# One product of 256 columns for the scores, and another order of a step's work in attention

## The reference, cut

```python
q = rmsnorm(q, q_norm_w); k = rmsnorm(k, k_norm_w)
q = apply_rope(q, rope_cos, rope_sin); k = apply_rope(k, rope_cos, rope_sin)
scores = einsum('bhtd,bhsd->bhts', q, k) * scale
scores = LOGIT_SOFTCAP * tanh(scores / LOGIT_SOFTCAP)
scores = where(mask, -inf, scores)
attn = softmax(scores, axis=-1)
out = einsum('bhts,bhsd->bhtd', attn, v)
return out @ wo.T
```

## Time and profile before

| | us |
|---|---|
| median of 3 runs | 2193.07 |
| lowest and highest | 2185.72, 2206.43 |
| the profiled execution, its own time | 2193.82 |
| its span in the trace | 2192.1 |
| PE busy, and PE weight loads | 2042.5 (93%), 1828.2 (83%) |
| DVE, ACT, POOL busy | 1085.6 (50%), 949.4 (43%), 1039.2 (47%) |
| granted TensorE clock, mean | 0.975 |

### The profile page before, as it was taken

One profiled execution on the slowest core, in us unless ns is written; L12 is line 12 of the kernel. 1 busy time (PEld: TensorE's weight loads), 2 busy tenths in 40 slices (PEclk: granted clock), 3 DMA queues, 4 the chain that ended last, 5 costly groups with the idle time before them and its releaser, 6 DMA issues.

```text
span 2192.1 us, 41896 instructions
## 1 busy us (share of the span) xinstructions
PE 2042.5 (93%) x12188; PEld 1828.2 (83%) x12189; DVE 1085.6 (50%) x2355; ACT 949.4 (43%) x2127; POOL 1039.2 (47%) x1070
## 2 busy tenths in 40 slices
PE   3999999999999999999968997899999999999997
PEld 2888888888888888888857886889999999988886
DVE  5555545555667676767545546333333333332322
ACT  4555545554565565656534410233333333333322
POOL 3444434442444445454546206367643223588864
PEclk9999999999999999999878998999999999999999
DMA  8877767777777776756324226467544333489898
GB/s 311 291 247 250 245 227 242 257 240 278 270 260 260 291 266 238 275 205 231 113 84 166 87 86 218 153 215 252 198 139 143 119 118 120 153 201 201 191 189 211
DMA packets 189240, 451.53 MB, mean 206 GB/s; under 512 B 21696, under 2 KB 21952, under 8 KB 189120
## 3 DMA queue, kind: packets, MB, share of 16 engines
q1 hardware_dynamic: 135648, 339.73, 45.3%
q0 software_dynamic: 21504, 51.13, 9.9%
q10 hardware_dynamic: 31968, 59.12, 8.4%
HBM read 276.41 MB, written 173.48 MB: 205 GB/s over the span
## 4 chain that ended last, share of the span: by engine, by line
PE 81%; issue 4%; DMA 3%; DVE 3%; ACT 3%; POOL 3%; SPq 0%; ACTq 0%; POOLq 0%
PE bank L1170 19%; PE bank L1046 13%; PE bank L1180 10%; PE bank L1094 8%; PE bank L1064 6%; PE bank L178 5%; PE bank L730 5%; PE bank L1112 3%; PE bank L740 3%; PE bank L1076 3%; PE bank L747 2%; POOL ex L1353 1%; PE bank L1104 1%; PE bank L478 1%; DMA xT<-xT_ffn 1%
## 5 line engine op out<-in xcount | busy, mean ns | idle before, releaser
L1170 PE MATMUL bank<-w_hi,xT 128*128 x1776 | 477.4, 331 | 19.3 <-issue 17.5
L1046 PE MATMUL bank<-w_hi,xT 128*128 128x512 f32 x1024 | 355.9, 409 | 13.8 <-DMA xT<-xT_att 9.3
L1170 PEld LDWEIGHTS bank<-w_hi,xT 128*128 128x128 f32 x1776 | 316.0, 188 | 42.2 <-issue 40.3
L1339 POOL TENSOR_TENSOR rr<-rr,expo 128x4 f32<-128x4 f32 x128 | 128.9, 1007 | 417.7 <-DVE rr L1456 417.7
L757 DVE TENSOR_TENSOR hT<-bank,hT 128x384 fp32r<-128x384 f32 x143 | 79.7, 557 | 439.2 <-ACT hT L754 439.2
L1170 PE MATMUL bank<-w_lo,xT 128*128 x888 | 286.6, 323 | 0.0
L1046 PEld LDWEIGHTS bank<-w_hi,xT 128*128 128x128 f32 x1024 | 197.8, 193 | 55.3 <-issue 13.2
L1180 PE MATMUL bank<-w_hi,hT 128*128 x666 | 229.5, 398 | 2.1 <-DVE hT L757 2.1
L754 ACT ACTIVATE hT<-bank 128x384 fp32r<-128x384 f32 x143 | 70.2, 491 | 341.8 <-PE bank L747 341.4
L1064 PE MATMUL bank<-w_hi,xT 128*128 128x256 f32 x1024 | 213.6, 292 | 0.0
L1094 PE MATMUL bank<-w_hi,oT 128*128 128x512 f32 x512 | 193.5, 419 | 20.0 <-DVE qkT L1451 18.3
(11 more groups left out here) (228 smaller groups left out, 4535.8 us busy)
## 6 DMA issues: line engine op xcount, KB each, us to landing
xT<-xT_att SPq DMA_DIRECT2D x128, 512.0 KB, 4.1
w_hi<-w_split SPq DMA_DIRECT2D x64, 512.0 KB, 6.6
w_lo<-w_split SPq DMA_DIRECT2D x64, 512.0 KB, 7.4
xg<-blank SPq DMA_DIRECT2D x111, 264.0 KB, 4.4
yg<-blank SPq DMA_DIRECT2D x111, 256.0 KB, 4.6
raw<-in_weights SPq DMA_DIRECT2D x88, 272.0 KB, 3.0
w_split<-w_hi SPq DMA_DIRECT2D x64, 272.0 KB, 3.4
w_split<-w_lo SPq DMA_DIRECT2D x64, 272.0 KB, 3.4
```

The costliest lines, as they stand in the source:

```text
L1046: last = pe.matmul(bank[par][:, :], xT[:, par, a, c * P:(c + 1) * P], w_hl[w][:, fw, c * 512:(c + 1) * 512], start=n == 0, stop=n == 11)
L1170: last = pe.matmul(out_[:, 0:I], xT[:, par, a, c * P:(c + 1) * P], flat(w_hl[w])[:, bass.ds(at + (c * 2 * I + half_ * I), I)], start=n == ...
L1339: pool.tensor_tensor(rr[:, :], rr[:, :], expo[:, :], ALU.pow).then_inc(pw_done, 1)
```

## The change

For each head, k's high part is loaded once as weights and meets q's high and low parts in one product of 256 columns; k's low part meets q's high part in a second product, which adds to the first 128 of these columns. So 4 products per tile take the place of 6. The bank `S_` then holds, for each head, two halves of 128 columns, and VectorE adds them into `th`, from which ScalarE's tanh reads and to which it writes.

The order inside a step changes too. TensorE does the transposes of `on` first after the Q and K projection, one step later than before, and PV behind Wo, just before S. ScalarE does `oT` high and `qkT` high before `sq`. VectorE does `oT` low and `qkT` low first, then `ssq` and `rr`, then the sum into `xres`, the new sum of the halves, and only then `rden`, `on`, `rot`, `vE` low. In the layer norm's helper two semaphores are merged into one.

```diff
@@ TensorE
+                    if tail:
+                        pe.wait_ge(on_done, s - 2)
+                        wait(pe, oT_lo, s - 3)
+                        for h in range(HG):
+                            last = pe.transpose(OT_[:, h * T:(h + 1) * T], on[:, h * DH:(h + 1) * DH], ident[:, :])
+                        last.then_inc(ot_done, 1)
                     if mid:
 
                         pe.wait_ge(k_out, s)
...
-                    if back:
-
-                        pe.wait_ge(p_hi, s - 1)
-                        pe.wait_ge(p_lo, s - 1)
-                        pe.wait_ge(v_hi, s - 1)
-                        pe.wait_ge(v_lo, s - 1)
...
                         last.then_inc(wo_done, 1)
                     if back:
 
-                        pe.wait_ge(on_done, s - 1)
-                        if tail:
-                            pe.wait_ge(oT_lo, s - 2)
+                        pe.wait_ge(p_hi, s - 1)
+                        pe.wait_ge(p_lo, s - 1)
+                        pe.wait_ge(v_hi, s - 1)
+                        pe.wait_ge(v_lo, s - 1)
...
                     if mid:
                         pe.wait_ge(qkT_hi, s)
                         pe.wait_ge(qkT_lo, s)
-                        wait(pe, th_done, 2 * s - 2)
+                        wait(pe, s_sum, s - 1)
                         for h in range(HG):
-                            for n, (a, w) in enumerate(TERMS):
-                                last = pe.matmul(S_[:, h * T:(h + 1) * T], qkT[:, a, (HG + h) * T:(HG + h + 1) * T],
-                                                 qkT[:, w, h * T:(h + 1) * T], start=n == 0, stop=n == 2)
+                            k_of, at = slice((HG + h) * T, (HG + h + 1) * T), 2 * h * T
+                            pe.matmul(S_[:, at:at + 2 * T], qkT[:, 0, k_of], qkT[:, :, h * T:(h + 1) * T],
+                                      start=True, stop=False)
+                            last = pe.matmul(S_[:, at:at + T], qkT[:, 1, k_of], qkT[:, 0, h * T:(h + 1) * T],
+                                             start=False, stop=True)
                         last.then_inc(s_done, 1)
@@ ScalarE
+                    if tail:
+                        act.wait_ge(ot_done, s - 2)
+                        act.activation(oT[:, 0, :, :], heads(OT_[:, 0:256]), ACT.Copy).then_inc(oT_hi, 1)
+                    if mid:
+                        act.wait_ge(t_done, s)
+                        act.activation(qkT[:, 0, :], QY_[:, :], ACT.Copy).then_inc(qkT_hi, 1)
                     if front:
                         act.wait_ge(qk_done, s + 1)
                         wait(act, ss_done, s)
                         act.activation(sq, bank[par][:, :], ACT.Square).then_inc(sq_done, 1)
...
-                        act.wait_ge(s_done, s)
+                        act.wait_ge(s_sum, s)
                         act.wait_ge(rms_done, s)
                         for h in range(HG):
-                            act.activation(th[:, h * T:(h + 1) * T], S_[:, h * T:(h + 1) * T], ACT.Tanh,
+                            act.activation(th[:, h * T:(h + 1) * T], th[:, h * T:(h + 1) * T], ACT.Tanh,
@@ VectorE
+                    if tail:
+                        dve.wait_ge(wo_done, s - 2)
+                        bb = behind(s, fw, b, 3)[1]
+                        dve.tensor_tensor(xres[:, bb, :], xres[:, bb, :], QY_[:, :], ALU.add).then_inc(acc_done, 1)
+                    if mid:
+                        dve.wait_ge(s_done, s)
+                        wait(dve, ex_done, s - 1)
+                        dve.reduce_sum(heads(th), S_[:, :].rearrange("p (h a n) -> p h n a", h=HG, a=2), AX.X)                            .then_inc(s_sum, 1)
                     if back:
                         dve.wait_ge(pv_done, s - 1)
```

More of the change, by code:

```diff
@@ L1067, in step @@
                         last.then_inc(v_done, 1)
-                    if back:
-                        pe.wait_ge(p_hi, s - 1)
-                        pe.wait_ge(p_lo, s - 1)
-                        pe.wait_ge(v_hi, s - 1)
-                        pe.wait_ge(v_lo, s - 1)
-                        for h in range(HG):
-                            for n, (a, w) in enumerate(TERMS):
-                                last = pe.matmul(O_[:, h * 130:(h + 1) * 130], pT[:, a, h, :],
-                                                 vE[:, par, w, h, :], start=n == 0, stop=n == 2)
-                        last.then_inc(pv_done, 1)
                     if rec:
@@ L1098, in step @@
                     if back:
-                        pe.wait_ge(on_done, s - 1)
-                        if tail:
-                            pe.wait_ge(oT_lo, s - 2)
+                        pe.wait_ge(p_hi, s - 1)
+                        pe.wait_ge(p_lo, s - 1)
+                        pe.wait_ge(v_hi, s - 1)
+                        pe.wait_ge(v_lo, s - 1)
                         for h in range(HG):
-                            last = pe.transpose(OT_[:, h * T:(h + 1) * T], on[:, h * DH:(h + 1) * DH], ident[:, :])
-                        last.then_inc(ot_done, 1)
+                            for n, (a, w) in enumerate(TERMS):
+                                last = pe.matmul(O_[:, h * 130:(h + 1) * 130], pT[:, a, h, :],
+                                                 vE[:, par, w, h, :], start=n == 0, stop=n == 2)
+                        last.then_inc(pv_done, 1)
                     if mid:
@@ L1221, in step @@
                         act.activation(sq, bank[par][:, :], ACT.Square).then_inc(sq_done, 1)
-                    if mid:
-                        act.wait_ge(t_done, s)
-                        act.activation(qkT[:, 0, :], QY_[:, :], ACT.Copy).then_inc(qkT_hi, 1)
                     if front:
@@ L1445, in step @@
                     front, mid, back, tail, rec = wants(s)
-                    if front:
-                        dve.wait_ge(sq_done, s + 1)
-                        dve.reduce_sum(ssq[:, :], sq.rearrange("p (g n) -> p g n", g=4), AX.X).then_inc(ss_done, 1)
+                    if tail:
+                        dve.wait_ge(oT_hi, s - 2)
+                        dve.tensor_tensor(oT[:, 1, :, :], heads(OT_[:, 0:256]), oT[:, 0, :, :].bitcast(F32),
+                                          ALU.subtract).then_inc(oT_lo, 1)
                     if mid:
@@ L1453, in step @@
                     if front:
+                        dve.wait_ge(sq_done, s + 1)
+                        dve.reduce_sum(ssq[:, :], sq.rearrange("p (g n) -> p g n", g=4), AX.X).then_inc(ss_done, 1)
+                    if front:
                         wait(dve, rms_done, s)
@@ L1476, in step @@
                                           vE[:, par, 0, :, 0:DH].bitcast(F32), ALU.subtract).then_inc(v_lo, 1)
-                    if tail:
-                        dve.wait_ge(wo_done, s - 2)
-                        bb = behind(s, fw, b, 3)[1]
-                        dve.tensor_tensor(xres[:, bb, :], xres[:, bb, :], QY_[:, :], ALU.add).then_inc(acc_done, 1)
-                    if back:
-                        dve.wait_ge(oT_hi, s - 1)
-                        dve.tensor_tensor(oT[:, 1, :, :], heads(OT_[:, 0:256]), oT[:, 0, :, :].bitcast(F32),
-                                          ALU.subtract).then_inc(oT_lo, 1)
                     if rec:
```

14 lines of the change are left out of this document (6 added, 8 removed).

## The result

The changed kernel takes 2239.48 us (median, 2235.25 to 2243.25) against 2194.89 before in the same sessions: the ratio is 1.0199, with a 95% interval of 1.0168 to 1.0230. It is slower by some 44 us; 2221 had been forecast. The interval ends just above 2%, so the loss itself is clear and its size is known to about 0.3%. The span grew from 2192.1 to 2238.1 us, by 46.0.

| | before | after | |
|---|---|---|---|
| first half of attention, steps 0 to 62 (first load of step 0 to that of step 63) | 485.5 | 493.7 | +8.2 |
| second half, with the recurrence (first load of step 63 to that of step 127) | 552.8 | 587.9 | +35.1 |
| all the rest | 1153.8 | 1156.5 | +2.7 |

A forecast was written before the change was run, and what follows sets the result against it. TensorE, 93% busy, was taken as the bound, with Wo nearly waiting for qkT. Plain steps 0, four recurrence pairs 19, first and last pairs 7, draining 1: +27 us on 2193.8, forecast 2221 us, range 2165 to 2250.

The forecast's parts named there:

- the product saves nothing: Rival: a 256-column weight read in two pieces costs 0.22 us, not 0.118; +26 us, 2247 us; chance 0.13.
- Plain steps: 62 steps without the recurrence: saving of 0.34 us becomes a 0.33 wait for qkT before Wo; 7.58 against 7.59, total 0.
- SyncE's queue keeps its order: Weight pieces: no DMA waited for in a new place; low part 0.7 us later, with over 3 us to spare.
- The step is 6.5 + R: Recurrence steps, if above a plain step's 7.6 us; R is the length of the recurrence's work on VectorE ahead of pT.
- r6: Recurrence step with a scan, then layer-norm statistics on VectorE: 11.1 us against 9.20, +1.9.
- r9: Recurrence step with 2.75 us of recurrence work on VectorE: 9.3 us against 7.86, +1.4.
- r5, r7, r8: Recurrence steps where ScalarE has 0.9 us of its own behind pT high: 8.2 or 8.3 us, +0.55 each.
- r0: Recurrence step with the layer-norm statistics alone: 8.2 us against 7.6, +0.6.
- r2, r3, r4: Steps with recurrence transposes between V and Wo or before the step: Wo does not wait, -0.33 us each.
- r1, r10: Steps bound by ScalarE's work behind a late GpSimd mask: +0.3 us for both, from -0.3 to +1.
- The saving stands: Rival: qkT is ready when V ends, so TensorE keeps its pace; taken as 2170 us; chance 0.17.
- The two cancel: Rival: VectorE's late cluster costs half, +13 us, and plain steps gain 0.1 each; 2201 us; chance 0.2.

The follow-up runs named there:

- product_qkt_first: Kernel before plus four products, sum of halves ahead of the sum into xres, and qkT ahead of sq and ssq: ratio 0.9971 to the kernel before.
- piece_first: Changed kernel with GpSimd's low part of the weight piece ahead of its power: ratio 1.0140 to the kernel before.
- order_alone: Changed kernel with the six products of before, tanh reading PSUM and no sum on VectorE: ratio 1.0179 to the kernel before.
- rot_first: Changed kernel with VectorE's rot ahead of the sum of the halves: one execution on a slower chip, only steps compared; r6 went from 10.68 to 9.74 us.
- product_alone: Kernel before with only the four products and VectorE's sum, in the old order: ratio 1.0101 to the kernel before.
- no_sum: Changed kernel without VectorE's sum; tanh reads 128 columns per head from PSUM, so scores lack k high by q low: ratio 1.0059 to the kernel before.
- halves_kept: Kernel before with four products, sum and qkT ahead of sq and ssq only in steps without the recurrence; other steps as before: ratio 0.9943.
- qkt_first: Kernel before with only ScalarE's qkT high ahead of sq and VectorE's qkT low ahead of ssq: ratio 1.0007 to the kernel before.

## Why the prediction was right, and where it was off

**S's price.** Forecast 0.46 us for four products, measured 0.46; the six transposes 0.76, measured 0.78; the sum 0.69, measured 0.69. A moving operand in two pieces costs no more than one in one piece. By the Trainium skill's isolated gap (TensorE: Matmul & The Clock Gate, "Back-to-back issue gap"), which that section itself gives for a single product, the four would have saved nothing. The trace disagrees: 0.46 against 0.67, and product_qkt_first has plain steps 0.22 shorter. That settles the rival "the product saves nothing".

**Plain steps.** Wo's load was put at 5.17 into the step and came at 5.14, with VectorE's `qkT` as what it waits for. The step was put at 7.58 and is 7.67: PV, placed behind Wo, takes 0.79 for its six loads (411.09 to 411.88) where it took 0.67 behind V. The mechanism was right and the term PV was taken from another neighbour. It is worth 0.08 in some 55 steps, 4 us. The margin of 0.31 us that the prediction gave the kernel before was really 0.19, since Wo loads 0.12 behind the end of `qkT` low.

**"SyncE's queue keeps its order ... the low part of a weight piece comes some 0.7 us later in a step that has over 3 us to spare."** This step failed. Before, in the step ahead of the earlier trace rows:

```profile
406.92 1.36 POOL L189 TENSOR_TENSOR w_lo<-raw,w_hi 128x544 fp32r<-128x544 f32 x1
```

The low part ended at 408.28, already 0.2 behind the start of the next step, so there were no 3 us to spare; for seven steps of eight nobody waits for it, but TensorE wants all pieces when a group changes. Those steps grew by 0.8 to 0.9, six times in the first half, 5 us, and piece_first took it back. This and the 4 us of PV make up the first half's 8.2, within a microsecond.

**The steps with the recurrence.** "The step is 6.5 + R" gave 11.1 for r6 and 9.3 for r9; measured 10.68 (when the clock held) and 9.06. In both steps the constant is 6.2 and not 6.5, mostly as the cluster ended 2.25 into the step and not 2.56. r5, r7, r8: put at 8.2 or 8.3, measured 8.31, 8.47, 8.46. r0: 8.2, measured 8.0 to 8.1. r3 and r4: -0.33 forecast, -0.2 measured at full clock, by the 0.12 of PV. The reason given was that the cluster `rden` to `vE` low moves behind S because the sum stands ahead of it. order_alone (r6 at 9.74 without the sum) and rot_first (r6 shorter by 0.94) show that for r6. In r9 VectorE's list and ScalarE's come out nearly level, so shortening the first alone gains nothing. What the prediction charged to r5, r7 and r8 only, the sum itself in the softmax chain, acts in most steps: product_alone has none of the new order and its r5, r7, r8 and r9 are 8.2 to 8.5 too. Its largest losses are in r10 and r1, 12.1 to 12.3 and 11.2 to 11.6 us against 10.0 and 9.4 to 9.8 before, where Wo comes 0.8 and 1.0 later and the clock falls behind it; they make 14 of its 28 us, and its r6 is 9.2 as before.

**The size.** The forecast for the four whole pairs (steps 75 to 118) was 19 us, and the timelines give 27.6; for the rest of the second half it was 7, and they give 7.5. The first half, put at 0, gives 8.2, and all outside of both, put at 1, gives 2.7. By place, over the four pairs:

| | forecast | measured |
|---|---|---|
| r6 | 7.6 | 11.1 |
| r9 | 5.6 | 4.7 |
| r5, r7, r8 | 6.4 | 7.2 |
| r0 | 2.4 | 1.8 |
| r2, r3, r4 | -4.0 | -1.4 |
| r1, r10 | 1.2 | 4.2 |

The term that was mis-sized is a wait of TensorE, counted at its own length. In three of the four pairs r6 takes 12.1 to 12.8 us instead of 10.7, and in three of the four r10 takes 3.8 to 4.1 us behind Wo instead of 2.53, at a mean clock of 0.50 to 0.64 there. That is 9 us together, as much as the whole gap. The wait itself hardly changed in r10: up to Wo TensorE stood 1.76 us before and stands 1.82 now, and before, the clock held in all four. What differs is the step ahead: in r9 TensorE was busy for 7.75 of 7.86 us before, and is for 7.61 of 9.06 now. That this decides it is argued, not shown. Since the clock can go either way in the same step, the nearness of 2221 to 2239 owes something to chance.

**The rivals.** "The saving stands" did not happen in the changed kernel, where `qkT` low would have had to end 0.3 us earlier. product_qkt_first has the saving, with PV still between V and Wo; in the new order it was not tested. "The two cancel" needed half of the cost in the second half; there was more, not less.

**Where the loss comes from, then.** In the second half, taking the sum out of the changed kernel gives back 26 us of 35 (no_sum). Product and sum together cost 20 in the new order (order_alone to the changed kernel) and 28 in the old one (product_alone). In the first half nothing is lost to the sum: with the sum in both, plain steps are 7.37 us in the old order with only `qkT` moved (product_qkt_first) and 7.67 in the new one, and the steps before a new group cost 4 to 5 us in either.

## What to carry to other kernels

An operation that takes work off the bounding engine may still sit in a chain that this engine waits for: price it where the chain is short of slack (here the softmax chain beside a recurrence), and apply it only in the stretches that have slack; halves_kept, 0.994 of the time before, is ahead of both kernels that way, though part of its gain is the loop's turn. When an operation is moved or delayed, look up who waits for it in the rarest step too: a piece that nobody misses in seven steps was the bound in the eighth. When a gain is read off a whole stretch, split it by step first: a third of the first half's gain here came from two steps out of 63, and no run tells why they were shorter. And before a wait is traded for a saving of the same length, look at what stands between producer and consumer: nothing in the computation asks for PV between V and Wo, but there it covered the time until `qkT` was ready.

## What the runs showed of the hardware

- Two r6 steps of one profiled execution, equal to the hundredth of a microsecond up to the end of TensorE's wait, went on at a granted clock of 1.00 in one case and at a mean of 0.61 in the other, 2.53 and 3.93 us for the same work. Waits in a dense matmul stretch have a price that comes and goes; it came behind a wait of 2.06 us too (r10, clock 0.58 behind Wo at 948.78). And step r3 ran at 0.82 before and 0.71 after with no wait in it.
- Six loads and products of 130 columns took 0.67 us behind products of 256 columns and 0.79 behind products of 512.
- Tanh of both heads took 0.70 us reading SBUF (changed kernel, at 413.32) and 0.63 reading PSUM, so it gained nothing from having the scores in SBUF.
- The mask on GpSimd took 0.75 us on average in the changed kernel and 0.97 before, since it mostly no longer runs beside VectorE's long instructions. In r6 it took 2.73 beside the scan before (876.92), 0.74 when it started 0.04 us ahead of the scan (906.96), and 2.47 in rot_first, where it started 0.47 behind it (910.32). This went in the change's favour.
- At the second pass of a loop of 16 steps one engine stood 3.6 us for nothing that the profile names, TensorE in the kernel before and VectorE in the changed one, and in product_alone none did. In qkt_first and order_alone it was TensorE again, 3.8 and 3.2 us.
